# Probabilities times values in four groups a batch instead of eight, in an attention and int8 feed-forward kernel

## The reference, cut to what matters

```python
qkv = encodings @ attn_w.T + attn_b                      # 16 x 256 x 384
scores = jnp.einsum('bhki,bhqi->bhkq', k, q) / math.sqrt(HEAD)
scores = jnp.where(mask, scores, NEG_INF)                # mask: key <= query
probs = jax.nn.softmax(scores, axis=2)                   # over the queries
combined = jnp.einsum('bhkq,bhkl->bhql', probs, v)
x = _layernorm(x + (out @ out_w.T + out_b))
acc = dot_general(round(x / x_scale), round(rhs / rhs_scale))
x = _layernorm(x + acc * x_scale * rhs_scale)
```

## Time and profile before

| | us |
|---|---|
| time, median of 3 runs | 286.72 |
| lowest, highest | 286.15, 288.01 |
| span of the profiled execution, first to last instruction | 285.2 |

### The profile page before, as it was taken

How to read it: one execution, slowest core, us unless ns; L and a number is a source line. 1 busy time by engine, 2 the same in 40 slices (tenths; PEclk the granted TensorE clock), 3 DMA queues, 4 the chain that set the end, 5 groups by cost and what they waited for, 6 DMA issues and landing times.

```text
span 285.2 us, 9729 instructions
## 1 busy us (share of the span) xinstructions
PE 239.1 (84%) x3259; PEld 173.3 (61%) x3259; DVE 226.7 (79%) x658; ACT 187.6 (66%) x434; POOL 109.6 (38%) x216
## 2 busy tenths in 40 slices
PE   2469798999898998979898979898998989898520
PEld 1326566777676776757676757676776767665310
DVE  7618878788888889798989898888889798984431
ACT  3121475777678596859687777779595867677641
POOL 7730304060717162424334261617162523242542
PEclk9999999999999999999999999999999999999955
DMA  3396292828182735455564728282736445101001
GB/s 92 125 224 116 80 203 77 190 85 180 59 196 89 172 107 151 77 161 98 162 116 140 138 86 192 74 200 79 165 75 173 84 156 87 38 8 37 18 18 37
DMA packets 50905, 32.54 MB, mean 114 GB/s; under 512 B 7260, under 2 KB 50876, under 8 KB 50876
## 3 DMA queue, kind: packets, MB, share of 16 engines
q1 hardware_dynamic: 50876, 32.18, 46.0%
HBM read 17.17 MB, written 14.68 MB: 112 GB/s over the span
## 4 chain that ended last, share of the span: by engine, by line
PE 48%; DVE 22%; DMA 11%; issue 10%; SPq 3%; ACT 2%; POOL 1%; DVEq 1%; ACTq 0%; POOLq 0%
PE pv_bank L861 11%; PE max_bank L817 10%; DMA k_stat<-imagek 7%; DVE part_max L644 7%; PE exp_bank L817 7%; DVE shift L680 5%; PE bank_b L897 4%; PE max_bank L820 3%; PE exp_bank L820 3%; PE bank_a L949 3%; DVE ffn L742 3%; PE bank_b L929 2%; DMA imagek<-qk_parts 2%; DVE shift L677 2%; PE bank_a L941 2%
## 5 line engine op out<-in xcount | busy, mean ns | idle before, releaser
L490 ACT ACTIVATE probs<-exp_bank 128x512 f32<-128x512 f32 (+1 forms) x192 | 101.3, 531 | 61.8 <-PE exp_bank L820 60.7
L644 DVE TRANSPOSE_TENSOR_REDUCE part_max<-max_bank 128x16 f32<-128x512 f32 (+1 forms) x192 | 116.9, 617 | 20.2 <-PE max_bank L820 18.8
L817 PE MATMUL max_bank<-q_move,k_stat 124*128 124x128 bf16 (+3 forms) x512 | 70.2, 239 | 20.6 <-DVE part_max L644 16.0
L817 PE MATMUL exp_bank<-q_move,k_stat 128*128 128x128 bf16 (+3 forms) x512 | 66.9, 233 | 0.7 <-DMA q_move<-shift 0.7
L817 PEld LDWEIGHTS max_bank<-q_move,k_stat 124*128 124x128 bf16 x512 | 39.7, 117 | 42.0 <-DVE part_max L644 21.4
L861 PE MATMUL pv_bank<-probs,v_stat 128*32 128x256 f32 (+3 forms) x1024 | 61.1, 311 | 0.0
L820 PE MATMUL max_bank<-causal,identb 128*128 128x128 bf16 (+1 forms) x192 | 46.0, 240 | 0.0
L820 PE MATMUL exp_bank<-causal,identb 128*128 128x128 bf16 (+1 forms) x192 | 45.5, 237 | 0.0
L430 POOL TENSOR_TENSOR qk_rest<-qk_f,qk_parts 128x512 f32<-128x512 f32 x15 | 17.4, 1163 | 72.5 <-ACT qk_f L506 72.5
L817 PEld LDWEIGHTS exp_bank<-q_move,k_stat 128*128 128x128 bf16 x512 | 42.0, 114 | 2.6 <-DMA q_move<-shift 1.2
L452 POOL TENSOR_SCALAR rstd<-moments 128x2 f32<-128x2 f32 x32 | 6.1, 191 | 78.3 <-DVE moments L757 69.1
(11 more groups left out here) (84 smaller groups left out, 332.8 us busy)
## 6 DMA issues: line engine op xcount, KB each, us to landing
imageq<-qk_parts SPq DMA_DIRECT2D x32, 192.0 KB, 1.9
imagek<-qk_parts SPq DMA_DIRECT2D x32, 192.0 KB, 2.0
q_move<-imageq SPq DMA_DIRECT2D x32, 192.0 KB, 4.1
k_stat<-imagek SPq DMA_DIRECT2D x32, 192.0 KB, 4.4
xt_in<-xt_dram SPq DMA_DIRECT2D x16, 128.0 KB, 2.2
x_in<-x_dram SPq DMA_DIRECT2D x16, 128.0 KB, 2.4
out_dram<-o SPq DMA_DIRECT2D x16, 128.0 KB, 1.9
q_move<-shift SPq DMA_DIRECT2D x32, 8.0 KB
```

Of the source, the lines that this page charges most:

```text
L490: act.activation(probs[u][:, 0:cols], exp_bank[u % EXP_BANKS][:, 0:cols], ACT.Exp, scale=SCALE).then_inc(exp_done[1], 1)
L644: dve.tensor_reduce(o32, max_bank[u % MAX_BANKS][:, 0:n * (TOK - key)].rearrange("k (c q) -> k c q", q=32), op=ALU.max, axis=AX.X, apply_t ...
L817: pe.matmul(tiles[:, j, :], keys, q_move[b.ring][0:rows, p0 + j, key:TOK], start=(j == 0), stop=False, skip_group_check=True)
```

## The change

The eight groups of a batch become four. The products of a group are the same as before, in the same order; the steps at which they are issued change with the groups.

| step of the phase | before | after |
|---|---|---|
| u0 (of the next batch's phase) | units 8, 9 | units 6, 7, 8, 9 |
| u1 | unit 10 | - |
| u2 | unit 11 | units 10, 11 |
| u5 | units 0, 1 | units 0, 1, 2, 3 |
| u6 | units 2, 3 | - |
| u7 | unit 4 | units 4, 5 |
| u9 | unit 5 | - |
| u10 | units 6, 7 | - |

```diff
-PV_GROUPS = [(0, 1), (2, 3), (4,), (5,), (6, 7), (8, 9), (10,), (11,)]
+PV_GROUPS = [(0, 1, 2, 3), (4, 5), (6, 7, 8, 9), (10, 11)]
@@ in pv
-                                         tiles_of(probs[u], u)[:, j, :], start=(n == 0), stop=(key == 3 * KB),
+                                         tiles_of(probs[u], u)[:, j, :], start=(u < 2), stop=(key == 3 * KB),
@@ in phase of TensorE
                     if u == 0:
-                        pv(b - 1, 5)
+                        pv(b - 1, 2)
                         turn_maxima(b, 1)
                         feed_forward(b - 3)
-                    if u == 1:
-                        pv(b - 1, 6)
                     if u == 2:
-                        pv(b - 1, 7)
+                        pv(b - 1, 3)
...
                     if u == 5:
                         pv(b, 0)
                     if u == 6:
-                        pv(b, 1)
                         turn_maxima(b + 1, 0)
                         turn_heads(b - 1)
                     if u == 7:
-                        pv(b, 2)
+                        pv(b, 1)
                     if u == 8:
                         project_qk(b + 3)
                         project_out(b - 1)
-                    if u == 9:
-                        pv(b, 3)
                     if u == 10:
-                        pv(b, 4)
                         turn_zq(b - 2)
```

## The result

| | before | after |
|---|---|---|
| time, median of 4 runs | 286.62 us | 291.79 us |
| lowest, highest | 286.15, 288.01 | 289.98, 292.25 |
| span of the profiled execution | 285.2 us | 290.0 us |

The ratio is 1.0147 (95% interval 1.0109 to 1.0185), and the two medians stand 1.8% apart: slower, and above the range of the prediction (281.0 to 290.0). The ratios of this document leave out runs that are over 1.5% slower than the fastest of their kernel; as these also have a lower granted clock, which is what the experiments are about, the medians given are those of all runs, and runs left out are named.

What follows compares the result with a forecast made beforehand. Bound: the loop through projection, ScalarE's copies, GpSimd and VectorE's shift, 15.18 us a period. Projection +1.5, collision +1.1, two slips -0.5 and tail -2.1 sum to 0.0: 286.7 us, no difference, range 281.0 to 290.0.

Steps and rivals of the forecast that it cites:

- The projection: TensorE's projection at u8, on the loop: 0.11 us later a period, 13 times, +1.5 us.
- A: Start of unit 4's max scores, where TensorE stops for VectorE in every period, 1.23 us idle; times are counted from it.
- my two bounds: A further unit in a group costs streaming alone, 0.105 us per 64 columns, or also pays its fixed 0.15 us again.
- TensorE's saving: TensorE's own work over all steps of a batch: 0.69 us less.
- The tail: Last three phases, where nothing is projected and TensorE is the path: 2.1 us gained.
- the collision: VectorE's earlier image copies meet GpSimd's power (L454) and lengthen its chain: +0.10 us a period, 11 periods, +1.1 us.
- the loop: From A through TensorE's projection, ScalarE's copies, GpSimd, VectorE's shift and max unit 2 back to TensorE: 15.18 us, the whole period.
- the turns of the loop: Two turns where GpSimd has 0.35 us more: VectorE may slip through ahead of L434, -0.5 us.
- The savings at u9, u10 and u1: TensorE's 0.35, 0.66 and 0.45 us saved there lie beside GpSimd's 5.40 us and its wait: counted as no gain.
- Rival 2: Larger collision: L658 and L659 hold L452 and L454, up to 0.45 us in 11 periods: 291.1 us, chance 0.18.
- Rival 1: Loop through GpSimd not closed tightly, VectorE's blocked time follows VectorE: 0.26 to 0.37 us less a period, 281.3 us, chance 0.17.
- Rival 3: TensorE's sum is the bound, so 0.69 us a batch counts in full: 11 us, 275.7 us, chance 0.05.

Runs made afterwards that it cites:

- a_fill6: Changed kernel with six matmuls that nothing reads put into TensorE's idle time ahead of unit 4: 289.46 us, ratio 1.0101.
- a_fill6_mid: Changed kernel with the six unread matmuls ahead of unit 4 only in phases 3 to 12: 288.21 us, ratio 1.0002.
- early: Kernel before with only the first half's groups changed (units 0 to 3 at u5, 4 and 5 at u7): 293.98 us, no ratio given.
- late: Kernel before with only the second half's groups changed (units 6 to 9 at u0, 10 and 11 at u2): 288.39 us, ratio 1.0009.
- a_poolwait: Changed kernel with GpSimd's residual sum and bias sum waiting until VectorE's shift is made: 274.93 us, ratio 0.9576.
- b_poolwait: Kernel before with GpSimd's residual sum and bias sum waiting until VectorE's shift is made: 275.34 us, ratio 0.9592.
- a_norm_after: a_poolwait with GpSimd's first normalisation factors (L452 to L458) moved behind L434: 271.15 us, ratio 0.9441.
- b_norm_after: b_poolwait with GpSimd's first normalisation factors (L452 to L458) moved behind L434: 272.98 us, ratio 0.9502.
- b_idle: Kernel before with products of units 8 to 11 cut to their first 8 query columns, to open idle time: 287.66 us, ratio 1.0026.
- early_poolwait: early with GpSimd's residual sum and bias sum waiting until VectorE's shift is made: 275.42 us, ratio 0.9557.

## Why the prediction was wrong

**Right, with its size.** The group of units 0 to 3 at u5: 0.90 us forecast, 0.90 measured (145.90 to 146.80). Units 4 and 5 at u7: 0.48 and 0.47 (84.07 to 84.54). Units 6 to 9 at u0: 0.79 and 0.78 (89.19 to 89.97). The projection: A+5.38 and A+5.39. So a second unit inside a group costs streaming alone, the lower of my two bounds. TensorE's saving: 0.69 us a batch by the sum, 0.63 between the two busy times of a period (13.97 in the earlier trace rows, 13.34 after). (A slip of 0.1 us in the sum over the run: 13 x 0.11 is 1.4, not 1.5.) The tail: 2.1 us forward, 2.4 measured; the timeline of ScalarE after has the copy that was at the earlier trace rows, 2.4 us nearer to A of phase 13 (271.48 - 237.88 = 33.60, and 266.69 - 230.72 = 35.97 before):

```profile
271.48 0.60 ACT L524 ACTIVATE heads_t<-pv_bank 128x512 f32<-128x512 f32 x1
```

**Right in kind, off in size: the collision.** +0.10 us a period was taken, with bounds 0 and +0.39; it is +0.19 (L430 to L434 3.05 against 2.86), and by another operation than I named. GpSimd and VectorE after:

```profile
153.35 1.17 POOL L430 TENSOR_TENSOR qk_rest<-qk_f,qk_parts 128x512 f32<-128x512 f32 x1 [3.09 <-ACT qk_f L506]
...
154.56 0.43 DVE L658 CAST qk_parts<-qk_rest 128x512 bf16<-128x512 f32 x1
154.61 0.43 POOL L452 TENSOR_SCALAR rstd<-moments 128x2 f32<-128x2 f32 x1
154.90 0.29 DVE L659 COPY qk_parts<-qk_parts 128x512 bf16<-128x512 bf16 x1
...
155.12 0.69 POOL L454 TENSOR_TENSOR rstd<-rstd,minus_half 128x2 f32<-128x2 f32 x1
...
156.41 1.17 POOL L434 TENSOR_TENSOR qk_parts<-qk_rest,qk_parts 128x512 bf16<-128x512 f32 x1
156.55 1.06 DVE L677 CAST shift<-shift_f 128x32 bf16<-128x32 f32 x1
...
157.65 1.34 DVE L680 TENSOR_TENSOR shift<-shift_f,shift 32x32 bf16<-32x32 f32 x2
158.22 0.72 POOL L442 TENSOR_TENSOR xb<-x_in,bo_sum 128x256 f32<-128x256 f32 x1
```

L658 starts 0.05 us ahead of L452, which then takes 0.43 us; L454 behind it is at its 0.69. L680 still ends 0.05 us behind L442 (158.99, 158.94): the end of the loop as read. The period that follows, 15.18 + 0.11 + 0.19 = 15.48, is the one measured where the clock was full, 15.44 to 15.49; one is 15.30, where L454 was held up a little (0.76) and L452 not, and L434 came 2.88 behind L430.

**Right here, and in part luck: the turns of the loop.** I took two slips of VectorE past GpSimd for -0.5 us together; they were 0.57 each against the kernel before, once the low clock's 1.57, which both of these periods have, is taken off. All engines after, at the first:

```profile
126.18 1.16 POOL L434 TENSOR_TENSOR qk_parts<-qk_rest,qk_parts 128x512 bf16<-128x512 f32 x1 [0.24 <-issue]
126.21 1.86 DVE L680 TENSOR_TENSOR shift<-shift_f,shift 32x32 bf16<-32x32 f32 x2
...
127.98 0.73 POOL L442 TENSOR_TENSOR xb<-x_in,bo_sum 128x256 f32<-128x256 f32 x1
```

L680 here starts beside L434, not behind it, and ends at 128.07, ahead of L442's end. The slip isn't firm: `a_fill6` has it at one of its two turns (a period of 15.02; the other is 15.58), and `a_fill6_mid` not at the one that the late image left undisturbed (15.69).

**The step that failed** is the sentence "The savings at u9, u10 and u1 lie beside GpSimd's 5.40 us and its wait, so they are hidden", which priced them at nothing. The prediction itself forecast that the idle time at A would grow "from 1.23 to about 2 us", and asked nothing further of it. A saving on an engine that waits becomes idle time, and this idle time has a price: in four of ten periods TensorE came out of it at half its clock, straight into the 5.3 us between A and the projection that the loop runs through, 1.57 us each. That is 6.3 us of a difference of 4.8. By the runs: with the idle time at A filled, no filled A is followed by the low clock, and the ratio is 1.0002; the profiled executions of `early` and `late` have six and two such periods and spans of 293.5 and 286.1 us; the kernel before gets it too, once its idle time is long enough; and with the loop opened and the idle time at A at 1.00 us or less the change costs nothing that can be told (0.9576 against 0.9592). Everything else on the prediction's account, put together, came out some 1.5 us better than its 0.0 in this execution, 0.6 of which are the turns.

**The rivals.** Rival 2's 291.1 us is close to the 291.8 measured, and would have been the wrong lesson: its mechanism cost 0.19 us a period, below the 0.33 from which it was to decide. Rival 1 (the loop not tight) holds only at the two turns of the loop; `a_poolwait` and `b_poolwait` show that the loop was closed by GpSimd everywhere else. Rival 3 would need the loop opened twice, as `a_norm_after` and `b_norm_after` do, and even then, with TensorE the bound in `b_norm_after`, it is 1.8 us, not 11. That the lower clock wasn't among the rivals at all is the real omission. The trace of the kernel before had given no example of it in its middle: at idle times of 1.18 to 1.51 us its clock is 1.00 throughout. That is one execution; whether others of that kernel, whose mean granted clocks on the three chips of the experiments run from 0.964 to 0.976, had such a stretch isn't shown.

## What to carry to other kernels

When an edit takes work from an engine that waits, its saving isn't "hidden", it is longer idle time: on TensorE, write down how long the idle stretch will be, compare it with the longest after which the trace of before still shows the full clock, and if it will be longer, price what stands behind it on the critical loop at the lower clock. Before work is taken from a nearly busy engine, look for the loop that sets the period; here one wait in GpSimd's order was worth 4%, and the whole edit at most 0.7%, and only after that loop had been opened. And when the total comes out near a rival's number, check that the rival's own term has its size.

## What the runs showed of the hardware that was not expected

**The clock after short idle times.** Over the profiles of before, after, `early`, `late`, `b_idle` and the unfilled A of `a_fill6_mid`, I counted the idle times at A from 76 to 241 us. Between 1.00 and 1.69 us there are 31, and none was followed by the lower clock. Between 1.70 and 1.95 us there are 24, and 14 were. In that band the length doesn't decide alone: 1.95 us did it at 95.09 after the change and not at 191.65, 1.70 us did it once in `early`. Each time the clock, still at 1.00 at A, then stood at 0.50 for about 3.4 us, and a projection on the loop came 1.51 us late with the old groups at u5, 1.57 with the new. What else decides is open; I didn't try it.
The Trainium skill ("TensorE: Matmul & The Clock Gate", section "HAM oscillation — how this bites in real kernels") tells of a kernel in which a wait of some 3 to 5 us for DMA, between bursts of matmuls, puts the engine back to half its clock each time, so that every burst starts cold. The traces here agree in kind but differ in size: the waits, for VectorE, were only 1.70 to 1.95 us, and 14 of 24 did it.

**Who waits at the shared ports.** Where VectorE's L658 starts 0.05 us ahead, GpSimd's L452 takes 0.43 in place of 0.19 us. VectorE's two L680 take 0.40 us alone, 1.34 beside L465 and L442, and 1.86 beside L434 and L465. The power (L454) is another matter. All engines in `early_poolwait` (its L659 and L660 are L658 and L659):

```profile
146.10 0.38 DVE L659 CAST qk_parts<-qk_rest 128x512 bf16<-128x512 f32 x1
146.15 0.89 POOL L454 TENSOR_TENSOR rstd<-rstd,minus_half 128x2 f32<-128x2 f32 x1
146.40 0.28 DVE L660 COPY qk_parts<-qk_parts 128x512 bf16<-128x512 bf16 x1
```

The cast, first by 0.05 us, holds L454 up (0.89 in place of 0.69), but the copy then runs its whole 0.28 us inside L454, as fast as where GpSimd does nothing (0.28 at 102.68 in `a_norm_after`). The kernel before has the same for the cast, which starts inside the L454 of the earlier trace rows (149.67 to 150.42) and still takes 0.38:

```profile
150.00 0.38 DVE L658 CAST qk_parts<-qk_rest 128x512 bf16<-128x512 f32 x1
```

The Trainium skill ("SBUF — State Buffer", section "Who interferes with whom") says that whoever comes first has the shared ports until its instruction is done, and the other is blocked until then. L452 and L680 agree with it, and so does L454 behind the cast; the cast and the copy inside L454 don't: where this GpSimd instruction comes first, it doesn't hold VectorE up for the duration that the profile gives.
